# A fused gated block on one core: spare expert tiles read in place by register, and the order of mask chunks, softmax rows and copies

## The reference, cut to what matters

```python
x = x + tanh(g_xattn[0]) * L0_xattn(layernorm(x), ctx_512, ...)   # softmax of a normalised similarity
x = x + tanh(g_ffn[0])   * L0_ffn(layernorm(x), ...)              # 32 experts, top 1
x = x + tanh(g_xattn[1]) * L1_xattn(ctx_512, ...)                 # threshold at the 76th largest of each row
x = x + tanh(g_ffn[1])   * L1_ffn(layernorm(x), ...)              # 64 experts, top 8, and a shared expert
```

```python
w_q = clip(round(weight / 0.5), -1, 1)
y   = x @ (w_q * scale[:, None] * mask[e]).T     # times the row's softmax weight
```

## Time and profile before

| what | value |
|---|---|
| median of 3 runs | 405.51 us (404.76 to 406.37) |
| the profiled execution | 406.02 us, its span 404.3 us |
| PE busy | 358.7 us, 89% of the span |
| DVE, ACT, POOL busy | 272.6, 181.1, 163.0 us |
| granted TensorE clock, mean | 0.947 |

### The profile page before, as it was taken

How to read it: one execution, slowest core, us unless ns; L and a number is a source line. 1 busy time by engine, 2 the same in 40 slices (tenths; PEclk the granted TensorE clock), 3 DMA queues, 4 the chain that set the end, 5 groups by cost and what they waited for, 6 DMA issues and landing times. The chain is left out here.

```text
span 404.3 us, 7694 instructions
## 1 busy us (share of the span) xinstructions
PE 358.7 (89%) x2419; PEld 217.4 (54%) x2419; DVE 272.6 (67%) x711; ACT 181.1 (45%) x354; POOL 163.0 (40%) x180
## 2 busy tenths in 40 slices
PE   8987928643977899999899999969999999999995
PEld 2755426312644365546466666645665656656563
DVE  3999896999376585999784484557555555555454
ACT  3477736624744446544645446533323233332331
POOL 6937542437551349978699677220000000000000
PEclk9996967785999899999999999999999999999999
DMA  7899964686701444445355442004121221212211
GB/s 186 139 258 218 197 208 149 221 263 217 233 17 51 128 137 131 130 131 195 132 190 174 159 153 73 25 29 146 61 78 58 72 71 58 78 56 74 77 53 52
DMA packets 50346, 51.31 MB, mean 127 GB/s; under 512 B 6732, under 2 KB 41484, under 8 KB 50318
## 3 DMA queue, kind: packets, MB, share of 16 engines
q1 hardware_dynamic: 34430, 38.08, 30.0%
q0 software_dynamic: 9216, 6.29, 9.1%
q10 hardware_dynamic: 6672, 6.59, 5.1%
HBM read 44.13 MB, written 7.08 MB: 127 GB/s over the span
## 5 line engine op out<-in xcount | busy, mean ns | idle before, releaser
L1047 PE MATMUL bank<-early,gu 128*128 128x512 f16 x768 | 177.7, 381 | 3.0 <-DVE arena L1608 3.0
L1047 PEld LDWEIGHTS bank<-early,gu 128*128 128x128 f16 (+1 forms) x768 | 75.0, 98 | 83.0 <-issue 4.4
L499 ACT ACTIVATE arena<-arena 128x512 f16<-128x512 f32 (+1 forms) x66 | 41.6, 631 | 134.6 <-DVE arena L1624 133.8
L1074 PE MATMUL bank<-dp,arena 128*128 128x256 f16 (+1 forms) x768 | 94.2, 273 | 1.1 <-POOL arena L457 0.7
L1074 PEld LDWEIGHTS bank<-dp,arena 128*128 128x128 f16 x768 | 74.7, 98 | 23.5 <-POOL arena L457 2.7
L1608 DVE TENSOR_TENSOR arena<-arena,bank 128x512 f32<-128x512 f32 x64 | 43.9, 686 | 56.7 <-PE bank L1047 40.2
L457 POOL TENSOR_TENSOR arena<-arena 128x512 f16<-128x512 f32 (+1 forms) x33 | 38.3, 1161 | 51.1 <-ACT arena L499 51.1
L1624 DVE TENSOR_TENSOR arena<-arena,early 128x512 f32<-128x512 f32 x64 | 48.4, 756 | 7.5 <-DVE arena L1608 2.7
L740 ACT ACTIVATE arena<-bank 128x512 f32<-128x512 f32 (+1 forms) x66 | 38.7, 588 | 17.5 <-PE bank L1047 17.4
L406 POOL TENSOR_TENSOR gu<-stage,gu 128x512 f16<-128x512 f32 x32 | 39.0, 1219 | 7.4 <-ACT dp L499 7.4
L1634 DVE TENSOR_TENSOR arena<-arena 128x512 f16<-128x512 f32 (+1 forms) x33 | 22.8, 691 | 24.5 <-ACT arena L499 24.5
(11 more groups left out here) (184 smaller groups left out, 368.6 us busy)
## 6 DMA issues: line engine op xcount, KB each, us to landing
early<-token_weights SPq DMA_DIRECT2D x126, 128.0 KB, 2.9
stage<-in_gu_t SPq DMA_DIRECT2D x32, 256.0 KB
gu<-in_masks_t POOLq DMA_DIRECT2D x16, 256.0 KB, 22.5
stage<-in_dp_t SPq DMA_DIRECT2D x32, 128.0 KB
expert_rows<-arena ACTq DMA_DIRECT2D x12, 256.0 KB
dp<-gu SPq DMA_DIRECT2D x22, 128.0 KB, 2.3
routed_rows<-arena SPq DMA_DIRECT2D x1, 1536.0 KB, 17.5
arena<-routed_rows ACTq DMA_DIRECT2D x3, 512.0 KB, 5.1
```

The lines of the kernel that those rows point to most:

```text
L499: return nc.scalar.activation(dst, src, ACT.Copy, scale=scale)
L1047: last = mm(dst[:, :], w, x16[:, h, b, c, :], start=(k == 0), stop=(k == 3 * C - 1))
L1074: last = mm(dst, inter16[0:m, s, a, k * P:(k + 1) * P], w, start=(q is None and j == 0 and k % 2 == 0), stop=True, skip_group_check=True)
```

## The change

The spare copies go. PE reads the 15 owners of a half into registers itself (`spare_owners`), and `experts_spare` multiplies with each owner's weights where they lie in `m16`. Each spare tile is now a full 128-column weight window in `dp16` that is zero except for its own 32 columns, so that the four tiles of a block add up in one PSUM region: 32 matmuls of 128x128 by 256 a piece, one after another. DVE clears that buffer once at the start. `experts(h, p)` calls `experts_spare(h, p)` for p = 4 and 5, and `routed_rows(h, p)` calls `spare_rows(h, p)` for them. The lists of all engines change with it. "..." marks what is left out.

```diff
+        spare_zero = dp16[:, PAIRS // 2:, :, :].rearrange("p a b c -> p (a b c)")
+        spare_x = spare_zero.rearrange("p (k c s n) -> p k c s n", k=4, c=C, s=2)
+        own_x = spare_zero.rearrange("p (a j n) -> p a j n", j=4, n=P)[:, :, :, 0:CAP]
...
-            load_spares(0)
-            load_pair(4)
-            load_pair(5)
-            load_spares(1)
-            for q in range(6, 8):
+            for q in range(4, 8):
                 load_pair(q)
...
-            for q in range(4, 7):
-                low_half(q)
             rsqrt(4, HT)
+            low_half(4)
+            gather(1)
+            low_half(5)
+            low_half(6)
+            rsqrt(5, HT)
             low_half(7)
-            rsqrt(5, HT)
-            gather(1)
+            for t in range(HT, T):
+                add_rows(t)
...
-                if 4 <= n < 4 + HT:
-                    add_rows(n)
...
+            def spare_rows(h, p):
+                if h == 0:
+                    act.wait_ge(spare_set, 1)
+                else:
+                    act.wait_ge(y_ready, p + 1)
+                a = 4 * C * (p - E0 // 8)
+                copy(own_x[:, a:a + 4 * C, :, :], ps_xt[p % 2].rearrange("p (a j n) -> p a j n", j=4, n=CAP)
+                     ).then_inc(xt_copied, 1)
...
+            router_exp(0)
+            softmax_rows(1)
             sim1_rows(1, 0, 1)
-            router_exp(0)
             high_half(2)
-            tanh_rows(0)
             high_half(3)
             load_rows(0)
-            softmax_rows(1)
+            router_rows(1)
+            norm_rows(1, 4, 5, 6, 7)
             routed_rows(0, 0)
...
-            router_rows(1)
-            norm_rows(1, 4, 5)
...
-            norm_rows(1, 6, 7)
             expert_rows(0, 3)
             routed_rows(0, 5)
             store_rows(0, 3)
-            router_exp(1)
+            load_rows(1)
+            tanh_rows(0)
             expert_rows(0, 4)
...
+            router_exp(1)
             high_half(4)
-            high_half(5)
-            load_rows(1)
-            weigh_rows(0, 1, 2, 3)
             routed_rows(1, 0)
...
             store_rows(1, 1)
+            weigh_rows(0, 1)
...
             store_rows(1, 2)
+            weigh_rows(2, 3)
...
-            high_half(6)
...
             store_rows(1, 5)
+            high_half(5)
+            high_half(6)
             mix_rows(0)
             high_half(7)
+            weigh_rows(4, 5, 6, 7)
...
-                if n == 3:
-                    weigh_rows(HT, HT + 1)
-                if n == 5:
-                    weigh_rows(HT + 2, HT + 3)
...
+            def spare_owners(h):
+                pe.wait_ge(owner_set, h + 1)
+                owner[:] = [pe.value_load(spare_e[0:1, h, j:j + 1], min_val=0, max_val=E0 - 1) for j in range(SPARE)]
+            def experts_spare(h, p):
+                n = PIECES * h + p
+                pe.wait_ge(xt_copied, n + 1)
+                for k in range(2):
+                    first = 2 * p + k - E0 // 4
+                    for i in range(8 * C):
+                        j, c, s = i // (2 * C), i // 2 % C, i % 2
+                        e = owner[min(4 * first + j, SPARE - 1)]
+                        last = mm(ps_y[p % 2][:, k * D:(k + 1) * D], spare_x[:, first, c, s, 96 * j:96 * j + P],
+                                  m16[:, bass.ds(e, 1), c, :].rearrange("p e o -> p (e o)"),
+                                  start=(i == 0), stop=(i == 8 * C - 1))
+                last.then_inc(y_ready, 1)
...
-            sim1(1, 0, 1)
-            keep_busy(4, bank[0][:, :])
+            keep_busy(8, bank[0][:, :])
             ranks(0)
...
             owners_of(0)
-            keep_busy(36, bank[0][:, :])
+            sim1(1, 0, 1)
+            spare_owners(0)
+            keep_busy(20, bank[0][:, :])
+            router_x((2, 3))
+            keep_busy(4, bank[0][:, :])
+            router(1)
+            keep_busy(4, bank[0][:, :])
             routed_x(0, 0)
...
             experts(0, 5)
+            spare_owners(1)
             keep_busy(8, bank[0][:, :])
...
             experts(1, 5)
-            keep_busy(10, bank[0][:, :])
             symmetric(0, 0)
+            keep_busy(24, bank[0][:, :])
             symmetric(0, 1)
...
+            v.memset(spare_zero.bitcast(F32), 0.0).then_inc(spare_set, 1)
...
-            for m in range(2, MB):
+            for m in range(2, 5):
                 mask_weights(m)
             similarity_rows(1)
             weights_of_rows(0)
-            find(4)
+            for m in range(5, MB):
+                mask_weights(m)
             attend(1)
...
-            thresholds(HT * need_of - used[0] - 8)
+            thresholds(HT * need_of - used[0] - 20)
...
             rows_ask(0)
-            thresholds(2)
+            thresholds(4)
             rows_affine(0)
+            thresholds(10)
             rows_mix(0)
```

More of the change, by code:

```diff
@@ L83, in flamingo_block @@
         rows16 = arena[:, 0:4096].rearrange("p (k s n) -> p k s n", k=T, s=2)
-        more = arena[:, 4096:8192].rearrange("p (j c o) -> p j c o", c=C, o=D)
-        wov = [[dp16[:, PAIRS // 2 + j, :, :] for j in range(SPARE)],
-               [more[:, j, :, :] if j < 8 else dp16[:, j + 1, :, :] for j in range(SPARE)]]
         silu = arena[:, 0:2048].bitcast(F32).rearrange("p (s n) -> p s n", s=2)
@@ L225, in flamingo_block @@
         row_out = sem("row_out")
-        wov_in = [sem(f"wov_in{h}") for h in range(2)]
         xs_in = [[sem(f"xs_in{h}_{j}") for j in range(3)] for h in range(2)]
@@ L277, in load_pair @@
                 sp.dma_start(stage_dn[s], dp_d[:, q, :]).then_inc(stage_in[s], 16)
-            def load_spares(h):
-                sp.wait_ge(owner_set, h + 1)
-                sp.wait_ge(mask_ready, MB)
-                for j in range(SPARE):
-                    e = sp.value_load(spare_e[0:1, h, j:j + 1], min_val=0, max_val=E0 - 1)
-                    sp.dma_start(wov[h][j], m16[:, bass.ds(e, 1), :, :].rearrange("p e c o -> p (e c) o")
-                                 ).then_inc(wov_in[h], 16)
             sp.dma_start(wk_sb[0:DC, :], wk_t).then_inc(attn_in, 16)
@@ L567, in high_half @@
                     act.wait_ge(y_ready, PIECES)
-                if q == 9:
+                if q == 10:
                     act.wait_ge(y_ready, 2 * PIECES)
@@ L965, in experts @@
                     pe.wait_ge(y_copied, n - 1)
-                if p == E0 // 8:
-                    pe.wait_ge(wov_in[h], 16 * SPARE)
+                if p >= E0 // 8:
+                    experts_spare(h, p)
+                    return
                 pe.wait_ge(xt_copied, n + 1)
@@ L1116, in _ @@
             routed_x(0, 2)
+            ranks(1)
             experts(0, 1)
             routed_x(0, 3)
-            router_x((2, 3))
+            owners(1)
             experts(0, 2)
             routed_x(0, 4)
-            router(1)
-            experts(0, 3, 0)
-            ranks(1)
-            experts(0, 3, 1)
+            owners_of(1)
+            experts(0, 3)
             routed_x(0, 5)
-            owners(1)
-            experts(0, 4, 0)
-            owners_of(1)
-            experts(0, 4, 1)
+            experts(0, 4)
             experts(0, 5)
+            spare_owners(1)
             keep_busy(8, bank[0][:, :])
@@ L1542, in _ @@
             choose(0)
-            find(2)
+            find(1)
             assign_spares(0)
@@ L1558, in _ @@
             choose(1)
-            find(2)
+            find(3)
             assign_spares(1)
@@ L1651, in _ @@
                 find(4 if n in (2, 3, 4) or n > 8 else 3)
-                if 7 <= n < 7 + HT:
-                    rows_stats(n - 3)
-                if n == 10:
+                if 4 <= n < 4 + HT:
+                    rows_stats(n)
+                if n == 8:
                     rows_ask(1)
-                if n == 13:
+                if n == 11:
                     rows_affine(1)
```

16 lines of the change are left out of this document (9 added, 7 removed).

## The result

The changed kernel is slower: 416.77 us (median of 4 runs, 414.54 to 418.80) against 405.94 (4 runs beside it), ratio 1.027 [1.021, 1.033]. In two later comparisons on other chips it was 1.011 [1.005, 1.017] and 1.021 [1.015, 1.027]. Some executions of any of these kernels run in a slower state; the ratios leave them out, the medians do not, and the profiles of f_exp_first_no_reads and r_changed_third are of that state. The forecast was 409.2 with a range of 401.5 to 413.5: right in sign, outside the range.

The account below looks back on a forecast made before the run. PE was taken to bound the kernel from about 136 us, waiting for others before 123.42. FFN start +4.9 less 1.2 for holes gave +3.7 on 406.0, 409.7, median 409.2; range 401.5 to 413.5.

Parts of the forecast that it names:

- E: End of half 1's experts on PE: 108.39 in the kernel before, forecast 107.7, 0.7 earlier.
- The reads: PE's 15 owner register reads per half: 0.48 each, 7.2 us a half, in which PE issues nothing.
- the 0.65 that was named as a sign of being wrong: Prediction's test on PE's register reads: wrong if each takes under 0.35 or over 0.65 us.
- The clearing: DVE clearing the 4096-word buffer at the start: at most 5.4 us, at most 1.0 of it late, taken as 0.
- the mask product of 4.40: One slow DVE mask product beside POOL's low halves; reordering might win 3.7 more; cost taken 0, bounds -1 and +2.
- F - E: Stretch from half 1's experts' end to the last FFN's start: 15.0 us before, forecast 20.6; under 19 means wrong.
- F: Start of the last FFN, first matmul of shared_step: 123.42 before, forecast 128.3, 4.9 later.
- third rival: Nothing behind E binds: fillers run beside late adjacencies, F about E + 18 to 19, 406 to 407; chance 0.12.
- pair 7: ACT's high_half(7) waits for pair 7, loaded from E + 11.0, landing 3.0 later; prep_rows thus starts at E + 17.0.
- POOL's and ACT's holes: In the last FFN, add_rows and weigh_rows leave its steps; POOL's holes go, 0.69 and smaller, 1.2 us together.
- Cheap reads: Rival: PE pays only the loads, 4.1 us a half, giving 403.4; chance 0.33.
- Dear reads: Rival: 0.82 us a read on PE, 5.2 more a half, giving 419.6; chance 0.15.

Follow-up runs that it names:

- f_exp_first_no_reads: Changed kernel with router_exp(1) ahead of load_rows(1) and constant addresses for spare experts' weights, no register reads: 410.04 us, 0.997.
- r_changed_third: The changed kernel itself, unaltered, run again on a further chip: 415.27 us, 1.021 against the kernel before.
- r_changed_again: The changed kernel itself, unaltered, run again on another chip: 414.97 us, 1.011 against the kernel before.
- a: Changed kernel with half 1's router exponentials, router_exp(1), moved ahead of load_rows(1) in ACT's list: 413.89 us, 1.013 against the kernel before.
- l: Kernel before up to half 1's experts, changed kernel's order from there on, without register reads: 1.016 against the kernel before.
- m: l with POOL's add_rows(4 to 7) moved behind low_step(1, 0): 1.013 against the kernel before.
- n_m: m with 8 instead of 20 threshold searches held back in DVE's list: 408.90 us, 0.997 against the kernel before.
- j: a with each owner's register read right ahead of its four matmuls, not 15 in a row: 422.86 us, 1.033 against the kernel before.
- b: a with tanh_rows(0) also moved ahead of load_rows(1) in ACT's list: 414.67 us, 1.013 against the kernel before.
- e: Kernel before with only ACT's weigh_rows(0 to 3) moved behind store_rows(1, 1) and store_rows(1, 2): 412.14 us, 1.008.
- k: e with POOL's reciprocal roots ahead of its low halves and ACT's high_half(6) behind store_rows(1, 5): 411.34 us, 1.011 against the kernel before.
- c: b with 10 fillers ahead of both symmetrics instead of 24 between them: 418.45 us, 1.022 against the kernel before.
- p: k with 44 fillers instead of 14 behind symmetric(0, 1): 410.38 us, 1.004 against the kernel before.
- q: n_m with 26 fillers instead of 14 behind symmetric(0, 1): 406.28 us, 0.998 against the kernel before.
- g: a with POOL's add_rows(4 to 7) moved behind low_step(1, 0): 1.010 against the kernel before.

## Why the prediction was wrong

**E came as forecast (107.7, measured 108.2), by luck: errors that met.** The reads were mis-sized: 0.48 each, 7.2 a half, against 0.68 and 10.2, over the 0.65 that was named as a sign of being wrong. The step "0.44, with the steps between them 0.48" took medians of instructions for the pitch of a sequence. "In which PE issues nothing" was wrong the other way, since the first reads run beside matmuls issued before: the pauses were 7.24 and 8.48, and half 1's experts started 1.9 later than forecast (94.41 for 92.5). Against that, the six pieces from the first expert to E took 13.8, not 15.2, since they ran at the higher clock. A spare matmul took 0.112 (forecast 0.109), `keep_busy(8)` 3.59 (3.6), the copies no longer stood behind `weigh_rows`. The clearing took 3.47 and the mask product of 4.40 did not come back (0.69 at most), both inside their bounds.

**F - E was the failed step: 20.6 forecast, 26.3 measured.** That is the execution profiled beside the forecast; in r_changed_again it was 19.0 and E was the late one, 114.1 for 107.7. Point by point, from E:

| | forecast | measured |
|---|---|---|
| both symmetrics and the fillers done | 9.0 | 13.2 |
| `rsqrt` starts | 12.9 | 16.2 |
| first copy of `prep_rows` | 17.0 | 20.0 |
| F | 20.6 | 26.3 |

The first line is 4.2 over; the next two give 1.2 back, and the last adds 2.6. The words of the first were "PE now does 1.75 of `symmetric`, 24 fillers at 0.228 = 5.5, and 1.75 of `symmetric`": PE's own time alone, with DVE not asked. DVE had stood 14.24 for the exponentials, whose move I had passed over, and PE waited 2.70 and then ran the second symmetric mostly at half clock (+1.6). I said of every moved step what it costs its own queue, and not of this one who waits for it. Only the third rival speaks of late adjacencies, and as a reason for a gain. The runs widen that: with the exponentials earlier (a) or in time (l, m) the adjacency is still late, because DVE also waits for rows that POOL has not added (5.37, 5.23 and 7.34), with searches held behind. n_m has neither late exponentials nor reads and holds 8 searches back; there PE does not wait for the adjacency, and the time is that of the kernel before. The changed kernel with its reads, its exponentials first and 8 searches held back was not run, so how the loss divides between the exponentials, the reads and the hold-back stays open.

**Two terms that I did count were not there.** `rsqrt` came 2.98 behind the second symmetric, DVE's 3.0 alone: POOL had been free from 120.1 on, the 0.9 for its queue was nothing. And pair 7 did not hold ACT: its copies ran at 122.45, `weigh_rows` from 123.29, `prep_rows` waited for PE. In its place the normalisations took 3.38 beside POOL's subtractions and adds, work that I had counted for its queue and not for its neighbour. The last line, from `prep_rows` to F, "3.64 as before", was 6.2: the half clock behind PE's wait, and the low parts beside POOL.

**In the FFN** I gave 1.2 back for POOL's and ACT's holes, and 3.2 came; the same 3.2 stands in l. The boundary of the halves took 2.7 of it again by the clock. The whole miss of the profiled execution, 417.2 for 409.7, is then F (134.5 for 128.3, 6.2), the first steps up to down(0) (14.7 for 14.1, 0.6) and the boundary (2.7), less the 2.0 by which half 0 was better than counted: 7.5.

**The rivals.** Cheap reads were refuted by the pitch. Dear reads (0.82) were nearer than my 0.48, and their time, 419.6, nearer than my forecast, for another reason. The argument for the cheap ones, that PE's sequencer may run ahead of its array, holds for the first 2 to 3 us of a row of reads and hardly at all between groups of four matmuls (j). The third rival's F - E of 18 to 19 came in r_changed_again, with E 6 later than it had.

## What to carry to other kernels

When a step is moved back in one engine's list, name who waits for its output and what is queued behind that wait; here one line moved in ACT's list stopped DVE for 14 us. Moving it back uncovered the next waits. An engine's idle time is conserved until the last of its causes goes: taking one wait away (a, b, e, k) showed the next one, and only combinations (f, n_m) came back to the time of the kernel before. Work placed behind a wait to shorten another path must be sized for how late the engine is, and where an engine's wait can't be removed, a filler in front of it is nearly free and saves the clock behind it (b against c, and the rows of p). And read more than one execution before a step is blamed: here a second profile of the same kernel lost more than half of its time elsewhere.

## What was unexpected of the hardware

- A register read on PE: load 0.30, register operation 0.15 and assertion 0.02 by their rows, 0.68 from one to the next in a row of 15, and 0.50 added where a read stands between groups of four matmuls. The first 2 to 3 us of such a row ran beside matmuls issued before it.
- The Trainium skill's DMA: Bandwidth & Descriptors page ("Latency and other measured facts") gives about 600 ns for a tensor_load. The instruction's row has a median of 301 ns here, so for the instruction the measurement decides; a whole read has a pitch of 680 ns in a row of 15.
- The same idle of 3.20 us at the boundary of the halves left the granted clock at 1.00 before (266:270) and at 0.58 after (274:278). PE's first steps behind F show the same scatter: the step ahead of down(0) took 2.75 in p, 4.14 in q and 5.26 in n_m.
- DVE's f32 operations beside POOL's tensor_tensors took up to 3.2 times as long: 3.38 for 1.46 (four normalisations), 2.28 for 1.28 (two low parts), 1.53 for 0.48 (one adjacency product).
- ACT's gap of 3.7 us ("remote") stands in the kernel before too, at 80.3 to 84.0, in a pause; in a, b, c and r_changed_again it stood on the path, and in the first profile of the changed kernel and in g it is absent. What it is was not settled.
